# Moving accumulations and D*u between engines in a fused selective-scan and FFN layer

## The reference

```
u, gate = split(xn @ W_in.T)                    # 1024 channels each
u   = silu(causal_conv4(u) + conv_b)
dt, B, C = rmsnorm of the parts of u @ Wx.T     # 32, 16, 16 columns
delta = softplus(dt @ Wdt.T + dt_bias)
state_t = exp(delta_t * A) * state_(t-1) + delta_t * u_t * B_t      # 1024 x 16 states
y_t = sum over n of state_t[:, n] * C_t[n]
s   = ((y + u * D) * silu(gate)) @ W_out.T
FFN(xn) = (silu(xn @ Wg.T) * (xn @ Wu.T)) @ Wd.T                    # 1376 wide
```

## Time and profile before

| | |
|---|---|
| median of 3 runs | 1162.8 us (1160.41 to 1163.04) |
| the profiled execution | 1162.58 us, of it 1160.5 us from the first to the last instruction |
| mean granted TensorE clock | 0.968 |
| busy: TensorE, VectorE, GpSimd, ScalarE | 1065.1, 1043.5, 985.8, 701.9 us |
| share of the chain that ended last | TensorE 46%, VectorE 22%, GpSimd 15%, ScalarE 6% |

### The profile page before, as it was taken

How to read it: one execution, slowest core, us unless ns; L and a number is a source line. 1 busy time by engine, 2 the same in 40 slices (tenths; PEclk the granted TensorE clock), 3 DMA queues, 4 the chain that set the end, 5 groups by cost and what they waited for, 6 DMA issues and landing times.

```text
span 1160.5 us, 14932 instructions
## 1 busy us (share of the span) xinstructions
PE 1065.1 (92%) x5072; PEld 760.4 (66%) x5072; DVE 1043.5 (90%) x1248; ACT 701.9 (60%) x1138; POOL 985.8 (85%) x555
## 2 busy tenths in 40 slices
PE   6989987989989999989999999999998999999767
PEld 4777665758567775666757776575857787555444
DVE  5599999997889999899989999899989999788895
ACT  5668446864665756667574856476575665465440
POOL 3487998999788899799988899889989899789961
PEclk9989997997999999999999999999999999999878
DMA  4657553632224544343324543343323443335310
GB/s 151 215 171 252 195 191 100 218 124 85 83 100 157 198 157 158 113 154 103 116 74 156 189 159 137 143 154 119 118 76 121 154 164 114 121 105 177 120 62 36
DMA packets 46550, 160.66 MB, mean 138 GB/s; under 512 B 5355, under 2 KB 5611, under 8 KB 37004
## 3 DMA queue, kind: packets, MB, share of 16 engines
q1 hardware_dynamic: 46332, 159.66, 39.9%
q10 hardware_dynamic: 144, 0.07, 0.0%
HBM read 135.33 MB, written 24.38 MB: 138 GB/s over the span
## 4 chain that ended last, share of the span: by engine, by line
PE 46%; DVE 22%; POOL 15%; issue 11%; ACT 6%; DMA 0%; SPq 0%; DVEq 0%; POOLq 0%; ACTq 0%
PE pj L1165 13%; DVE sb_h L1104 12%; PE hT L1454 9%; PE pj L1363 7%; POOL sb_dBu L840 7%; DVE sb_yT L1024 5%; PE pj L1397 4%; PE pj L1428 3%; PE pj L1183 3%; POOL sb_yT L800 3%; PE pj L1170 2%; PE pj L1472 2%; DVE sb_un L916 2%; POOL sb_un L771 1%; ACT dA L608 1%
## 5 line engine op out<-in xcount | busy, mean ns | idle before, releaser
L840 POOL TENSOR_TENSOR sb_dBu<-sb_v,sb_bb 128x1024 f32<-128x1024 f32 x254 | 603.3, 2388 | 37.5 <-DVE sb_h L1104 23.9
L1104 DVE TENSOR_TENSOR_SCAN sb_h<-dA,sb_dBu 128x512 f32<-128x512 f32 x512 | 598.0, 1212 | 24.3 <-POOL sb_dBu L840 16.0
L608 ACT ACTIVATE dA<-sb_delta,sb_apar 128x512 f32<-128x512 f32 x510 | 344.8, 688 | 251.5 <-DVE sb_h L1104 247.6
L1165 PE MATMUL pj<-sb_x_hi,sb_w_sp 128*128 128x512 f32 x1208 | 341.6, 406 | 16.2 <-DVE sb_un L916 12.7
L1454 PE MATMUL hT<-sb_ident,sb_h 128*128 128x128 f32 x2048 | 290.4, 284 | 60.0 <-DVE sb_yT L1024 49.1
L1454 PEld LDWEIGHTS hT<-sb_ident,sb_h 128*128 128x128 f32 x2048 | 244.8, 146 | 144.8 <-issue 49.8
L1024 DVE SCALAR_TENSOR_TENSOR sb_yT<-hT,sb_cs,sb_yT 128x512 f32<-128x512 f32 x335 | 239.5, 741 | 49.9 <-PE hT L1454 49.1
L1165 PEld LDWEIGHTS pj<-sb_x_hi,sb_w_sp 128*128 128x128 f32 x1208 | 218.5, 190 | 79.6 <-issue 25.1
L800 POOL TENSOR_TENSOR sb_yT<-sb_yT,sb_part 128x512 f32<-128x512 f32 x141 | 180.8, 1283 | 58.4 <-ACT sb_part L708 58.1
L708 ACT ACTIVATE sb_part<-hT,sb_cs_act 128x512 f32<-128x512 f32 x141 | 96.5, 684 | 138.0 <-PE hT L1454 135.9
L1165 PE MATMUL pj<-sb_x_lo,sb_w_sp 128*128 128x512 f32 x604 | 163.9, 393 | 0.0
(11 more groups left out here) (143 smaller groups left out, 807.9 us busy)
## 6 DMA issues: line engine op xcount, KB each, us to landing
sb_w_sp<-w_cache SPq DMA_DIRECT2D x55, 1024.0 KB, 4.8
sb_ring<-w_ring SPq DMA_DIRECT2D x67, 512.0 KB, 3.9
sb_bb<-b_rows SPq DMA_DIRECT2D x128, 256.0 KB, 4.0
w_cache<-sb_w_sp SPq DMA_DIRECT2D x19, 1024.0 KB, 4.9
sb_xio<-x SPq DMA_DIRECT2D x7, 1024.0 KB, 7.2
out<-sb_xio SPq DMA_DIRECT2D x3, 1024.0 KB, 5.8
sb_xio<-x SPq DMA_DIRECT2D x4, 256.0 KB, 3.4
out<-sb_xio SPq DMA_DIRECT2D x4, 256.0 KB, 2.0
```

The costliest lines, as they stand in the source:

```text
L608: nc.scalar.activation(dA[g % 2][:, :], delta[:, j, :], ACT.Exp, scale=apar[:, j, n:n + 1]).then_inc(dA_done, 1)
L840: nc.gpsimd.tensor_tensor(dBu[:, dbu_buffer(s), :, :], v[:, j:j + 2, :], bb[:, i % B_RING, :].unsqueeze(1).to_broadcast([P, 2, T]), ALU.mu ...
L1104: nc.vector.tensor_tensor_scan(h[:, i % 2, 2 * part + e, :], dA[g % 2][:, :], dBu[:, dbu_buffer(s), e, :], 0.0, ALU.mult, ALU.add).then_in ...
L1165: done = nc.tensor.matmul(bank[:, :], w[:, kk * P:(kk + 1) * P], xs[:, kk, :], start=(p == 0), stop=(p == len(products) - 1))
```

## The change

For sequences 1 to 3, VectorE accumulates five tiles itself that were handed over: (13, c=2), (14, 0), (14, 2), (15, 0), (15, 2). Five tiles that VectorE accumulated are handed over: c=1 of units 17 to 21. In all sequences the four pairs of D*u stand in ScalarE's slots 32, 33, 34 and 37 instead of 34 to 37. The number of handed-over tiles in a sequence stays 42; the `op_ps` wait goes with the first pair.

```diff
+UD_AT = {32: 0, 33: 1, 34: 2, 37: 3}
...
 def handed_over(u, first):
-    return () if u in (29, 30) or first and u < FIRST_UNIT else (0, 2) if 11 <= u < 23 else (0,)
+    if u in (29, 30) or first and u < FIRST_UNIT:
+        return ()
+    if not first and 13 <= u < 16:
+
+        return () if u > 13 else (0,)
+    if not first and 17 <= u < 22:
+        return 0, 1, 2
+    return (0, 2) if 11 <= u < 23 else (0,)
...
-                    p = s - 34
-                    if 0 <= p < PAIRS:
+                    if s in UD_AT:
+                        p = UD_AT[s]
                         if p == 0 and not first:
                             act.wait_ge(op_ps, b * KH)
                         for j in (2 * p, 2 * p + 1):
```

## The result

The changed kernel takes 1193.5 us, median of 4 runs (1190.05 to 1196.65), against 1162.9 us before: ratio 1.0269, 95% interval 1.0236 to 1.0302. The forecast was 1196. The profiled execution took 1196.65 us, with a span of 1194.7.

What follows compares the result with a forecast made beforehand. Bound in turn by TensorE, VectorE with GpSimd, then TensorE. Sum: 1162.6 + 0.6 (sequence 0) + 11.0 (late `conv_silu`) + 13.0 (clock) + 6.8 (last sequence) + 1.5 (its clock) = 1195.5, about 1196 us; range 1174 to 1204.

Steps and rivals of the forecast that it cites:

- scan of slot 33 late: VectorE's scan in sequence 1, slot 33, starts at 480.9 instead of 476.43, 4.5 us late, waiting for ScalarE's decays.
- scan of slot 36 late: VectorE's scan of slot 36 in sequence 1 comes 3.3 to 3.5 us late; 3.3 taken.
- GpSimd's stretch, length: GpSimd, `dBu` of slot 40 to end of eighth `conv_silu`: grows 2.2 us from 51.3 to 53.5, without idle time.
- eighth `conv_silu` late: GpSimd's eighth `conv_silu`, before the Wx projection, ends 3.3 + 2.2 = 5.5 us late in sequences 1 and 2: 11.0.
- TensorE idle before the projection: TensorE sits idle some 6.5 us before the Wx projection, having ended slot 46 with only transposes left.
- clock, sequences 1 and 2: TensorE's Wx projection falls mostly to 1.2 GHz, costing 6.5 us each, 13.0; rival that the clock holds: 0.17, 1181.
- last sequence, without and with the clock: Last sequence: 3.8 us from the `op_ps` wait plus 3.0 from GpSimd, 6.8; 1.5 more taken for TensorE's clock.
- sequence 0: Sequence 0, only D*u moves: `take_state` and the following rounding come 0.6 us later, GpSimd waits; bounds 0 and 1.3.
- The accumulations taken back cost 0: VectorE, slots 29 to 33: five accumulations hide in waits for TensorE's transposes; cost 0, at most 0.2 us.
- The op_ps wait: ScalarE's slot 32: first D*u pair waits until 478.9 for TensorE's slot 30, holding back slot 33's decays and VectorE's scans.
- VectorE's relief is lost to GpSimd: VectorE, slots 36 to 44: 3.2 us less work, without gain as GpSimd is next; rival that it counts: 0.05, 1156.
- The starting point: The sum starts from 1162.6 us, the profiled execution's own time, with the median within 0.3.

Runs made afterwards that it cites:

- both accumulation parts: Against the changed kernel, D*u put back in ScalarE's slots 34 to 37, both accumulation edits kept: 1182.2 us, ratio 1.0156 to the kernel before.
- the changed kernel with matmuls added: Changed kernel plus 512-column TensorE products before the Wx projection, 24 in sequences 1 and 2, 6 in sequence 0: 1179.4 us, ratio 1.0131 to before.
- taken back alone: Against the kernel before, only the five accumulations of units 13 to 15 go back to VectorE: 1163.9 us, ratio 0.9992.
- D*u alone: Against the kernel before, only D*u moves, to slots 32, 33, 34 and 37; accumulation table as before: 1172.6 us, ratio 1.0079.
- D*u from slot 33: Changed kernel, but with D*u in slots 33, 34, 35 and 37: 1178.7 us, ratio 1.0135 to the kernel before.
- handed over alone: Against the kernel before, only c=1 of units 17 to 21 goes to GpSimd; units 13 to 15 and D*u as before: 1182.8 us, ratio 1.0143.

## Why the prediction was right, point by point

| term | forecast, us | measured, us |
|---|---|---|
| scan of slot 33 late | 4.5 | 4.5 |
| scan of slot 36 late | 3.3 | 3.3 |
| GpSimd's stretch, length | 53.5 | 53.1 |
| eighth `conv_silu` late | 5.5 | 5.1 |
| TensorE idle before the projection | 6.5 | 5.5 |
| clock, sequences 1 and 2 | 6.5 each | 8.6 and 4.7 |
| last sequence, without and with the clock | 6.8, 8.3 | 6.1, 8.5 |
| sequence 0 | 0.6 | 0.9 by slot 36, in part chance |

- *The accumulations taken back cost 0.* Right, shown by running them alone.
- *The op_ps wait.* Right in place, length and in what stood behind it. Run alone, the D*u move costs 8.1 us in medians; in slot 33, a wait of 3.2 us is free.
- *VectorE's relief is lost to GpSimd.* Right: the scan of slot 45 has made up its lateness (193.43 against 193.40 us), as the 3.3 - 3.2 of the forecast say, and from slot 48 on VectorE waits for `dBu`. The stretch grew by 1.8 instead of 2.2 us: standing in a row an addition takes some 1.23 us from start to start, four take 4.9, and so 3.1 us of the stretch had been free, where the idle times add up to 2.8.
- *The clock.* Right that it falls in both sequences. That the sum of 13.0 met 13.3 is in part luck, as the price of one sequence is not a constant: the low clock lasted through both halves of the projection in sequence 1 and ended during the second half in sequence 2. The ground given was weak too: sequence 0 was taken as a sign of how little it takes, but with the same work and the same idle time (1.33 against 1.31 us) its projection kept 1.00 in the changed kernel. What sets sequences 1 and 2 apart is an idle time of 5.5 us, and there the fall came in every trace that has it. The idle time was worked out 1 us too long, and for the kernel with both accumulation parts 2.3 us too short, because I put it down to the late `conv_silu` alone. Where VectorE is relieved, TensorE is also early.
- *The last sequence.* The two delays are right: in the execution without the extra fall of the clock (the changed kernel with matmuls added) the scan of slot 36 is 4.2 us late (forecast 3.8), and GpSimd adds 2.9 by slot 51 (forecast 3.0); of these 7.2 the end keeps 6.1. The 1.5 for the clock was a choice within "up to 3" that no row supports, and it was put down to the longer idle time in slots 32 and 33. In the changed kernel's trace the clock made 2.4, of it 1.7 at slots 36 to 38, but there the trace with the accumulations taken back alone loses 1.5 as well, with D*u where it was. That 8.3 met 8.5 is luck.
- *Sequence 0.* The three kernels with D*u in slot 32 are 0.9 us late by slot 36 of sequence 0 (counted from slot 33), the six others 0 to 0.7. So the step costs something between 0.2 and 0.9; 0.6 can't be told from that.
- *The starting point.* The sum starts from a profiled execution that had a fall of the clock in sequence 0. The changed kernel's has none there but a slower start, and the two nearly cancel. That is luck, not forecast.
- *Do the terms add up?* In the traces they do: in sequences 1, 2 and last, D*u alone costs 9.9 us and both accumulation parts 22.8, together 32.7, and the changed kernel has 32.4. In medians D*u alone costs 8.1 us, both accumulation parts 17.7, together 25.8, and the changed kernel 30.6. The median of both accumulation parts is that of four runs from 1174.7 to 1188.6 us, and the slowest is the profiled one. That this spread explains the 4.8 us is likely, but not shown.

By its rule for elementwise work on two inputs (the Trainium skill, GPSIMD Engine Reference, Engine selection), GpSimd takes about twice VectorE's time. The runs here have 1.28 us for GpSimd's addition against 0.74 for VectorE's instruction, which multiplies and adds, a factor 1.73. The direction agrees, and the size goes by the measurement. What decided the GpSimd term was not this factor alone, but that the stretch had only 2.8 us of idle time.

## What to carry to other kernels

Before a wait is moved to an earlier slot, find where the signal comes and what stands behind the waiting instruction: one slot later the same wait was free. Work handed to another engine is free only up to that engine's idle time, in the stretch in which it sets the pace; here that was 2.8 us. One more addition fitted and gave 1.1 us a sequence, four more cost 2.1 to 2.2, and work taken from the engine ahead of the stretch gave nothing. If the engine in front of TensorE becomes late, or TensorE early, look at the granted clock of the matmuls that follow: in sequences 1 and 2 together the fall cost 13.3 us and the delay that brought it 10.5. And compare traces stage by stage: a match of two totals can hide differences of 6 or 7 us that cancel.

## What the runs showed of the hardware

After 5.5 to 5.9 us in which TensorE did nothing, the Wx projection ran at 1.2 GHz from its first matmul in sequences 1 and 2 of all four kernels that had such an idle time (the changed one, both accumulation parts, D*u from slot 33, handed over alone). How long the low clock lasted differed (20.5 and 13.7 us in the changed kernel). After 0.4 us (before, D*u alone, taken back alone) it kept 2.4 GHz each time. After 1.3 to 1.5 us, in sequence 0 of the seven kernels without added matmuls, it fell in two (1.4 us into the projection or later) and held in five. 24 products whose result is thrown away kept it at 2.4 GHz. They cost next to nothing in time (the projection starts 0.1 us later) and made the changed kernel 14.1 us faster, and its sequences 1 and 2, which do the same work, then took the same 276.0 us.
